# A four-block transformer kernel on one core: GpSimd's bias additions, the inner layer's readouts and the coupling's update as steps of their own, in a new order

## The chip, the core and the metric

The kernel runs on one core of a Trainium2 chip. The metric is the device time of one execution in microseconds (us); lower is better. The engines are TensorE (PE in the profile: matmuls; PEld: its weight loads), VectorE (DVE), ScalarE (ACT), GpSimd (POOL) and SyncE (SP), which issues the DMAs. Each takes its instructions in program order; they wait for each other by semaphores.

## What is computed

The input is 16 sequences of 512 tokens with 256 features, in fp32. Every sequence passes four blocks, each on a normalized input and added back to the state (the kernel folds the last block's factor 0.5 and the middle block's into its weights). Cut to what matters:

```
# L0_attn: latent attention, causal
kv_c = rms(x @ W_kv) * g_kv ; q_c = x @ W_q
k, v, q = kv_c @ W_kdec, kv_c @ W_vdec, q_c @ W_qdec        # 16 heads of 16
k_rope, q_rope = rope(x @ W_krope), rope(q_c @ W_qrope)     # 16 heads of 32
out = softmax(causal([q, q_rope] @ [k, k_rope].T * scale)) @ v @ W_o
# L0_ffn: three rounds of a coupling on the transposed state
for _ in range(3):
    tf = sigmoid(gelu(gelu(gelu(out @ w1 + b1) @ w2 + b2) @ w3 + b3) @ w4 + b4)
    coupling = 0.1 + adaptive_range * (0.7 * gf + 0.3 * tf - 0.5) * 2
    out = out + coupling * twist(out)
# L1_attn: attention with strided keys (strides 1 1 2 2 2 2 4 4 4 4 8 8 8 8 16 16),
#          then layer_norm, @ W1, relu, @ W2, layer_norm
# L1_ffn: s = x @ Win ; sum over 16 inner units of W2 * relu(W1 * s + b1) ; @ Wout + bout
```

The coupling block and the inner block come twice for each sequence: as A and C (coupling, on the input and behind the first attention) and as D and F (inner block, ahead of the second attention and at the end).

## The kernel before

A sequence is called q. Its state lies in X (four tiles of 128 tokens by 256 features), the normalized state in XN and its transpose in XT; each has three slots, for q modulo 3. The stages of a sequence are A (coupling), B (latent attention), C (coupling), D (inner block), E (strided attention), E2 (the two-layer part behind it) and F (inner block). Work of up to four sequences is interleaved: the string TURN lists the steps of one turn as `offset:name.stage.group.part`, and `all_steps` repeats it, turn t giving the steps of q = t + offset. There is no planner at run time: each engine walks through the same list and issues its own part of each step, so the order in TURN is the order on all five queues. A full turn holds every step of the kernel once, and its order decides which work of one sequence lies beside which of another. Where a step has no part for an engine, the engine skips it.

The steps that matter here:
- `xt`: TensorE turns XN (8 matmuls, L476), ScalarE copies it to XT. GpSimd also does the bias additions here, in `transposed` (L1229 on), as instructions over all four tiles: for D and F one (L1233), for E two (L1238, L1239), for E2 two (L1243, L1244). The signal `biased` tells VectorE of each.
- `h1`, `h2`, `h3`, `tf`: the four layers of the coupling net for one round; ScalarE reads out each. In the step `tf` VectorE also moves the state in XT in two halves (`mixed`, L824 to L828). `back` turns the moved state back.
- `stats`, `normal`: VectorE's statistics and normalization (L806, L796, L798, L815), with a power on GpSimd between them (L1217). `latent` and `centre` have such a power too.
- `turn`: a rotation (TensorE's product, VectorE's L865, L866, L868, GpSimd's sum L1254 and a rounded copy L1259); `content`: further products, copied by ScalarE (L1104, L1108, L1114) and rounded by GpSimd (L1268); `max`: scores for the row maxima, reduced by VectorE (L883, L889); `shift`: the maxima turned and subtracted (L895); `exp`: scores and exponentials (L1146), for B with a causal mask by GpSimd (L1275); `sum`: products with the values; `divide`, `att`, `proj`: their end. Banks 0 to 3 of PSUM, as two pairs taken in turn, serve `max`, `exp` and a part of `content` and `v`; banks 5 to 7 the rest.
- `inner`: one product on TensorE; ScalarE then reads it out eight times (L1172) and VectorE adds the eight up in `inner_sum` (L921, then L927 seven times), which ends in `g_ready`; `mout` on TensorE waits for that.
- `up`, `down`: E2's two layers. `down` has VectorE's additions (L949) and needs E2's bias addition; `centre` and `scale` (L960, L969) follow.

A step's name for one sequence is written below as in TURN, exp.B.2.3 for group 2 and key tile 3 of B. A turn that is shown is the one from 1809 to 2030 us of the span.

## Time and profile before

| | |
|---|---|
| median of 3 runs | 3766.49 us (3765.93 to 3772.34) |
| profiled execution, own time | 3778.47 us |
| its span, first to last instruction | 3776.5 us |
| granted TensorE clock, mean | 0.944 |
| TensorE / VectorE / ScalarE / GpSimd busy | 93% / 61% / 51% / 25% |

Busy time is the sum of an engine's instructions over the span. A wait is idle time of an engine ahead of an instruction, put down to whatever released it last. The granted clock is a share of TensorE's full speed of 2.4 GHz; 0.50 is the lower level, 1.2 GHz. In a timeline, neighbouring instructions of one kind are merged into a row, with their number as x; TensorE's rows overlap a little, so the work of a step is best read from one start to the next.

### The profile page before, as it was taken

The numbers are of one execution on the slowest core, as the hardware profiler recorded it, in microseconds if no ns is written. First come the engines' busy times: TensorE is split into PE (matmuls) and PEld (weight loads), VectorE is DVE, ScalarE is ACT, GpSimd is POOL, SyncE is SP. The second block draws the span as 40 slices with busy tenths as digits, with TensorE's granted clock in tenths as the row PEclk, the third lists the DMA queues.
The fourth block names the chain that finished last, engine by engine and source line by source line (L and its number), as shares of the span: only waits on it lengthen the run. The fifth ranks groups of instructions, "written<-read, shape, count | busy, mean of one in ns | idle before, by whom it ended". The sixth has DMA issues, their size and how long they took to land.

```text
span 3776.5 us, 63466 instructions
## 1 busy us (share of the span) xinstructions
PE 3513.1 (93%) x24928; PEld 1994.7 (53%) x24928; DVE 2296.3 (61%) x4778; ACT 1934.1 (51%) x3075; POOL 957.0 (25%) x1037
## 2 busy tenths in 40 slices
PE   5778999999999999999999999999999999999966
PEld 3344555555555555555555555555555565555443
DVE  3446565666756666675666667566666756566442
ACT  2244645546464554646455464645546465554522
POOL 2213132231313223131322313123231313323111
...
GB/s 90 1 1 1 1 1 12 1 12 1 10 3 1 12 1 12 1 7 7 1 12 1 12 1 1 12 1 12 1 12 1 1 12 1 12 1 7 1 6 6
DMA packets 40884, 27.74 MB, mean 7 GB/s; under 512 B 19601, under 2 KB 39697, under 8 KB 40593
## 3 DMA queue, kind: packets, MB, share of 16 engines
...
## 4 chain that ended last, share of the span: by engine, by line
PE 75%; DVE 19%; ACT 3%; issue 2%; POOL 1%; DVEq 0%; ACTq 0%; POOLq 0%
PE ps L465 67%; PE ps L476 7%; DVE G L927 3%; DVE XN L815 2%; DVE stats L806 2%; DVE MX L889 1%; DVE XN L868 1%; DVE MX L883 1%; DVE XN L865 1%; DVE X L969 1%; DVE XN L866 1%; DVE LT L855 1%; DVE mv L796 1%; DVE XN L960 1%; ACT L1146 1%
## 5 line engine op out<-in xcount | busy, mean ns | idle before, releaser
L1146 ACT ACTIVATE PR<-ps 128x1024 f32<-128x1024 f32 (+4 forms) x720 | 540.3, 795 | 604.9 <-PE ps L465 603.4
L465 PE MATMUL ps<-MAT 32*128 32x512 f32 (+5 forms) x4928 | 602.2, 520 | 68.0 <-ACT MAT L1108 52.1
L889 DVE TENSOR_REDUCE MX<-ps 128x2 f32<-128x1024 f32 (+3 forms) x512 | 392.2, 819 | 216.4 <-PE ps L465 214.2
L1217 POOL TENSOR_TENSOR rstd<-var,neg_half 128x4 f32<-128x4 f32 x144 | 150.1, 1042 | 1465.1 <-DVE var L798 1288.9
L465 PEld LDWEIGHTS ps<-MAT 32*128 32x128 f32 (+2 forms) x4928 | 275.7, 203 | 367.0 <-issue 237.5
L883 DVE TENSOR_REDUCE MX<-ps 128x2 f32<-128x1024 f32 (+6 forms) x256 | 219.7, 900 | 299.5 <-PE ps L465 299.5
L465 PE MATMUL ps<-XT,cn_w 128*128 128x256 f32 x1536 | 363.8, 390 | 11.5 <-DVE XT L826 10.8
L465 PE MATMUL ps<-other,cn_w 128*128 128x512 f32 (+2 forms) x1152 | 319.1, 481 | 14.9 <-ACT other L1066 7.6
L465 PEld LDWEIGHTS ps<-XT,cn_w 128*128 128x128 f32 x1536 | 289.7, 194 | 80.3 <-issue 22.4
L1275 POOL TENSOR_SCALAR_AFFINE_SELECT PR<-PR 128x512 f32<-128x512 f32 x256 | 178.9, 699 | 455.5 <-ACT PR L1146 455.1
L1254 POOL TENSOR_TENSOR MAT<-XN 128x512 f32<-128x512 f32 x128 | 163.7, 1279 | 478.4 <-DVE XN L868 478.4
L465 PE MATMUL ps<-HI 32*128 32x256 f32 (+4 forms) x3072 | 218.7, 374 | 45.1 <-DVE MX L889 23.8
L465 PE MATMUL ps<-XT,w_up 128*128 128x512 f32 x512 | 243.3, 610 | 1.0 <-ACT XT L1046 0.9
L815 DVE TENSOR_SCALAR XN<-X,mv,rstd 128x256 f32<-128x256 f32 x384 | 220.3, 635 | 25.3 <-POOL rstd L1217 23.9
L465 PE MATMUL ps<-w_down,other 128*128 128x256 f32 x1024 | 227.4, 380 | 0.0
L824 DVE TENSOR_TENSOR other<-other,XT 128x256 f32<-128x256 f32 x192 | 118.4, 617 | 171.8 <-ACT other L1089 171.8
L465 PEld LDWEIGHTS ps<-HI 32*128 32x128 f32 x3072 | 120.7, 197 | 179.7 <-issue 131.2
L465 PEld LDWEIGHTS ps<-w_down,other 128*128 128x128 f32 x1024 | 193.4, 190 | 33.8 <-issue 7.7
L1268 POOL CAST HI<-MAT 128x512 fp32r<-128x512 f32 (+3 forms) x256 | 156.3, 623 | 198.3 <-ACT MAT L1114 152.0
L1172 ACT ACTIVATE other<-ps,cols 128x512 f32<-128x512 f32 x256 | 174.9, 788 | 58.2 <-PE ps L465 58.2
L465 PE MATMUL ps<-XT,w_qk 128*128 128x512 f32 (+3 forms) x512 | 198.4, 535 | 0.8 <-ACT XT L1049 0.8
L465 PE MATMUL ps<-PR,VB 128*17 128x512 f32 (+3 forms) x2048 | 193.6, 457 | 1.5 <-POOL PR L1275 1.4
...
## 6 DMA issues: line engine op xcount, KB each, us to landing
...
```

The source lines that it names most:

```text
L465: return pe.matmul(dst, lhsT, rhs, start=start, stop=stop, skip_group_check=True)
L476: last = pe.transpose(dst[:, t * P:(t + 1) * P], src(t), ident[:])
L815: last = dve.tensor_scalar(XN[:, c, t, :], src[:, t, :], mv[:, c, t, 0:1], rstd[:, c, t:t + 1], ALU.subtract, ALU.mult)
L824: dve.tensor_tensor(WT[:, a, tok], TF[:, a, tok], XT[:, c, 1, tok], ALU.mult)
L883: last = dve.tensor_reduce(MX[:, t0:t0 + len(parts), at], src[:, :, 0:len(parts) * nk].rearrange("p j (t k) -> p t j k", k=nk), AX_X, ALU.max)
L889: last = dve.tensor_reduce(MX[:, t, at], src[:, :, a:a + nk[pair]], AX_X, ALU.max)
L1146: freed(act.activation(PR[0:m, tile_of((s, q, g, kt)), 2 * pair:2 * pair + 2, q0:T], ps[0:m, b:b + 2, 0:T - q0], ACT.Exp, scale=SCALE[s]), ...
L1172: last = act.activation(U[:, area_of[s], j, :], src, ACT.Relu, scale=c_mw1[:, j:j + 1], bias=c_mb1[:, j:j + 1])
L1217: pool.tensor_tensor(rstd[:, c, :], var[:, c, :], neg_half[:], ALU.pow).then_inc(rstd_ready.sem, 1)
L1254: pool.tensor_tensor(dst, a, b, ALU.add).then_inc(rope_sum.sem, 1)
L1268: pool.tensor_copy(HI[:, content_tile((s, q, g), w, hi=True), 0:n], MAT[:, content_tile((s, q, g), w), 0:n]).then_inc(hi_ready.sem, 1)
L1275: pool.affine_select(out=p, in_=p, compare_op=ALU.is_ge, fill=0.0, base=0, pattern=[[0, 4], [1, P]], channel_multiplier=-1).then_inc(maske ...
```

## The change

Three groups of work get steps of their own, and TURN is written anew with them.
- `bias`: GpSimd's additions leave `xt` and come as bias.D, bias.F, bias.E and bias.E2, each in two parts of two tiles (n = 0, 1). VectorE waits for part 1, and in `down` for the part that it needs. bias.E.1 comes in the next turn.
- `relu`: the eight readouts and sums of an inner layer leave `inner` and come as four steps of two each. `inner` is left with its product.
- `mix`: VectorE's movement of the state leaves `tf` and comes as two steps, one for each half.

Every arithmetic instruction stays, but for the additions of GpSimd, which are now 160 over 128x512 instead of 80 over 128x1024. All other steps keep their content; their order in TURN is new. The strided attention's first group keeps its four rounds of `max`. The string begins at another point of the turn, with the offsets moved along.

```diff
@@ -28,23 +28,27 @@
 MAT_TILES, HI_TILES = 8, 4
 
 TURN = """
--1:exp.E.2.0 1:h3.A.1 0:proj.B 0:stats.C 1:tf.A.1 -1:max.E.1.1 0:normal.C -1:content.E.0 1:h1.A.2 -1:shift.E.1
--1:max.E.0.0 1:h2.A.2 0:xt.C 1:h3.A.2 -1:sum.E.3.0 -1:max.E.0.1 1:tf.A.2 0:h1.C.0 -1:max.E.0.2 -1:divide.E.3
-1:back.A 1:stats.B -1:exp.E.1.0 0:h2.C.0 -1:max.E.0.3 -1:sum.E.2.0 0:h3.C.0 1:normal.B -1:exp.E.1.1 -1:shift.E.0
-0:tf.C.0 -1:sum.E.1.0 1:xt.B -1:exp.E.0.0 -1:divide.E.2 -1:sum.E.1.1 1:latent.B -1:exp.E.0.1 1:turn.B.0.k
--1:sum.E.0.0 -1:exp.E.0.2 -1:sum.E.0.1 1:kvt.B 1:turn.B.0.q 1:content.B.0 -1:exp.E.0.3 -1:divide.E.1 0:h1.C.1
-1:max.B.0.0 -1:sum.E.0.2 0:h2.C.1 1:max.B.0.1 -1:sum.E.0.3 0:h3.C.1 -1:divide.E.0 1:max.B.0.2 1:turn.B.1.k -1:att.E
-1:v.B 1:shift.B.0 0:tf.C.1 1:exp.B.0.0 -1:proj.E 1:turn.B.1.q 1:exp.B.0.1 0:h1.C.2 -1:stats.E2 1:content.B.1
-0:h2.C.2 -1:normal.E2 1:max.B.1.0 0:h3.C.2 -1:xt.E2 1:sum.B.0.0 0:tf.C.2 1:exp.B.0.2 -1:up.0 -1:up.1 1:sum.B.0.1
-1:max.B.1.1 -1:up.2 0:back.C 1:max.B.1.2 0:stats.D 1:sum.B.0.2 -1:up.3 -1:up.4 1:exp.B.0.3 1:shift.B.1 1:turn.B.2.k
-1:exp.B.1.0 1:sum.B.0.3 1:turn.B.2.q 0:normal.D 1:content.B.2 -1:up.5 1:exp.B.1.1 -1:up.6 1:max.B.2.0 0:xt.D -1:up.7
-1:divide.B.0 1:max.B.2.1 0:inner.D -1:down.0 1:max.B.2.2 -1:down.1 -1:centre 1:sum.B.1.0 1:exp.B.1.2 1:shift.B.2
--1:scale 1:sum.B.1.1 1:exp.B.1.3 -1:stats.F 0:mout.D 1:sum.B.1.2 1:exp.B.2.0 -1:normal.F 1:turn.B.3.k 1:sum.B.1.3
-0:stats.E 1:exp.B.2.1 1:sum.B.2.0 -1:xt.F 1:turn.B.3.q 0:normal.E 1:exp.B.2.2 -1:inner.F 1:content.B.3 1:sum.B.2.1
-1:exp.B.2.3 1:sum.B.2.2 1:max.B.3.0 -1:mout.F 1:max.B.3.1 0:xt.E 1:divide.B.1 1:sum.B.2.3 1:max.B.3.2 0:content.E.3
-1:shift.B.3 2:stats.A 2:normal.A 0:v.E 1:exp.B.3.0 0:content.E.2 1:exp.B.3.1 1:sum.B.3.0 2:xt.A 1:exp.B.3.2 2:h1.A.0
-0:max.E.3.0 1:divide.B.2 1:sum.B.3.1 1:exp.B.3.3 2:h2.A.0 0:shift.E.3 0:max.E.2.0 2:h3.A.0 1:sum.B.3.2 1:sum.B.3.3
-2:tf.A.0 0:content.E.1 0:exp.E.3.0 1:divide.B.3 2:h1.A.1 0:shift.E.2 0:max.E.1.0 1:att.B 2:h2.A.1
+1:xt.A -1:max.E.3.0 1:h1.A.0 0:exp.B.3.2 0:divide.B.2 1:h2.A.0 -1:shift.E.3 -1:max.E.2.0 1:h3.A.0 0:sum.B.3.1
+1:tf.A.0 0:sum.B.3.2 1:mix.A.0.0 0:exp.B.3.3 1:mix.A.0.1 -1:shift.E.2 -1:content.E.1 -1:exp.E.3.0 1:h1.A.1
+0:sum.B.3.3 -1:max.E.1.0 1:h2.A.1 0:divide.B.3 -1:content.E.0 1:h3.A.1 0:att.B -1:max.E.1.1 1:tf.A.1 1:mix.A.1.0
+0:proj.B -1:shift.E.1 1:mix.A.1.1 -1:exp.E.2.0 0:stats.C 1:h1.A.2 -1:max.E.0.0 0:normal.C -1:sum.E.3.0 1:h2.A.2
+-1:max.E.0.1 1:h3.A.2 -1:divide.E.3 0:xt.C -1:max.E.0.2 1:tf.A.2 0:h1.C.0 1:mix.A.2.0 1:mix.A.2.1 1:back.A 1:stats.B
+-1:max.E.0.3 0:h2.C.0 -1:sum.E.2.0 0:h3.C.0 -1:exp.E.1.0 1:normal.B -1:divide.E.2 -1:shift.E.0 1:xt.B -1:exp.E.1.1
+0:tf.C.0 0:mix.C.0.0 -1:sum.E.1.0 0:mix.C.0.1 -1:exp.E.0.0 -1:sum.E.1.1 -1:bias.E.1 1:latent.B 1:turn.B.0.k
+-1:exp.E.0.1 -1:sum.E.0.0 -1:exp.E.0.2 -1:sum.E.0.1 1:kvt.B 1:turn.B.0.q 1:content.B.0 -1:exp.E.0.3 0:h1.C.1
+-1:sum.E.0.2 1:max.B.0.0 0:h2.C.1 -1:divide.E.1 1:max.B.0.1 0:h3.C.1 -1:sum.E.0.3 0:tf.C.1 1:max.B.0.2 -1:divide.E.0
+1:turn.B.1.k -1:att.E 1:shift.B.0 1:v.B 0:mix.C.1.0 1:turn.B.1.q 0:mix.C.1.1 1:content.B.1 -1:proj.E 1:exp.B.0.0
+-1:stats.E2 0:h1.C.2 -1:normal.E2 1:max.B.1.0 1:sum.B.0.0 -1:xt.E2 0:h2.C.2 -1:up.0 0:h3.C.2 1:max.B.1.1 0:tf.C.2
+-1:up.1 0:mix.C.2.0 1:exp.B.0.1 -1:bias.E2.0 0:mix.C.2.1 -1:up.2 0:back.C 1:exp.B.0.2 1:sum.B.0.1 -1:up.3 0:stats.D
+1:max.B.1.2 1:sum.B.0.2 0:normal.D -1:up.4 1:exp.B.0.3 1:turn.B.2.k 1:sum.B.0.3 -1:up.5 1:shift.B.1 -1:up.6
+1:turn.B.2.q 1:exp.B.1.0 -1:up.7 1:content.B.2 -1:bias.E2.1 1:exp.B.1.1 0:xt.D 1:max.B.2.0 0:inner.D 0:relu.D.0
+1:divide.B.0 1:max.B.2.1 0:bias.D.0 -1:down.0 0:relu.D.1 1:max.B.2.2 0:relu.D.2 1:sum.B.1.0 0:relu.D.3 -1:down.1
+-1:centre 1:exp.B.1.2 -1:scale 1:sum.B.1.1 1:exp.B.1.3 0:bias.D.1 1:shift.B.2 -1:stats.F 0:mout.D 1:sum.B.1.2
+-1:normal.F 1:exp.B.2.0 1:sum.B.1.3 1:turn.B.3.k 0:stats.E -1:xt.F 1:exp.B.2.1 1:turn.B.3.q 0:normal.E -1:inner.F
+-1:bias.F.0 -1:relu.F.0 -1:relu.F.1 1:sum.B.2.0 1:content.B.3 -1:relu.F.2 1:exp.B.2.2 1:sum.B.2.1 -1:relu.F.3
+1:exp.B.2.3 0:xt.E -1:bias.F.1 1:max.B.3.0 -1:mout.F 1:sum.B.2.2 1:max.B.3.1 0:bias.E.0 0:v.E 1:divide.B.1
+1:max.B.3.2 0:content.E.3 1:shift.B.3 2:stats.A 1:sum.B.2.3 1:exp.B.3.0 0:content.E.2 2:normal.A 1:exp.B.3.1
+1:sum.B.3.0
 """
 
 
...
@@ -915,24 +918,26 @@
                     for n in range(2):
                         read_out(dve, "proj", s, q, n)
 
-                def inner_sum(s, q):
+                def inner_sum(s, q, i):
                     a = area_of[s]
-                    dve.wait_ge(inner_ready.sem, inner_ready.at(s, q, 0))
-                    link(dve.tensor_scalar(G[:, a, :], U[:, a, 0, :], c_mw2[:, 0:1], c_mb2, ALU.mult, ALU.add))
-                    for j in range(1, 8):
+                    for j in (2 * i, 2 * i + 1):
                         if j < 7:
                             dve.wait_ge(inner_ready.sem, inner_ready.at(s, q, j))
                         else:
                             read_out(dve, "s", s, q)
-                        last = dve.scalar_tensor_tensor(G[:, a, :], U[:, a, j, :], c_mw2[:, j:j + 1], G[:, a, :],
-                                                        ALU.mult, ALU.add)
+                        if j == 0:
+                            last = dve.tensor_scalar(G[:, a, :], U[:, a, 0, :], c_mw2[:, 0:1], c_mb2, ALU.mult, ALU.add)
+                        else:
+                            last = dve.scalar_tensor_tensor(G[:, a, :], U[:, a, j, :], c_mw2[:, j:j + 1], G[:, a, :],
+                                                            ALU.mult, ALU.add)
                         if j < 7:
                             link(last)
-                    last.then_inc(g_ready.sem, 1)
-                    dve.wait_ge(g_ready.sem, g_ready.at(s, q))
+                    if i == 3:
+                        last.then_inc(g_ready.sem, 1)
+                        dve.wait_ge(g_ready.sem, g_ready.at(s, q))
 
                 def features_added(s, q):
-                    dve.wait_ge(biased.sem, biased.at(s, q))
+                    dve.wait_ge(biased.sem, biased.at(s, q, 1))
                     for n in range(2):
                         src = when_full(dve, "mout", s, q, n).rearrange("p (t d) -> p t d", t=2)
                         x = X[:, q % CH, 2 * n:2 * n + 2, :]
...
@@ -942,8 +947,7 @@
 
                 def down_added(q, n):
                     c = q % CH
-                    if n == 0:
-                        dve.wait_ge(biased.sem, biased.at("HB", q))
+                    dve.wait_ge(biased.sem, biased.at("HB", q, n))
                     src = when_full(dve, "down", q, n).rearrange("p (t d) -> p t d", t=2)
                     acc = XN[:, c, 2 * n:2 * n + 2, :]
                     freed(dve.tensor_tensor(acc, src, acc, ALU.add), "down", q, n)
...
@@ -1166,14 +1170,15 @@
                             last = act.activation(ATT[:, f, :], src, ACT.Identity, bias=c_vb[:, f:f + 1])
                         freed(last, "att", s, q, f)
 
-                def inner(s, q):
+                def inner(s, q, i):
                     src = when_full(act, "s", s, q)
-                    for j in range(8):
+                    for j in (2 * i, 2 * i + 1):
                         last = act.activation(U[:, area_of[s], j, :], src, ACT.Relu, scale=c_mw1[:, j:j + 1],
                                               bias=c_mb1[:, j:j + 1])
                         if j < 7:
                             last.then_inc(inner_ready.sem, 1)
-                    freed(last, "s", s, q)
+                    if i == 3:
+                        freed(last, "s", s, q)
 
                 for name, *a in STEPS:
                     if name == "xt":
...
@@ -1226,22 +1231,20 @@
                     linked[0] += 1
                     pool.wait_ge(pool_step, linked[0])
 
-                def transposed(s, q):
-                    c = q % CH
+                def bias(s, q, n):
+                    x, xn = (t[:, q % CH, 2 * n:2 * n + 2, :] for t in (X, XN))
                     if s in "DF":
                         pool.wait_ge(xn_ready.sem, xn_ready.at(s, q))
-                        pool.tensor_tensor(X[:, c], X[:, c], bcast(bout_d), ALU.add).then_inc(biased.sem, 1)
-                    elif s == "E":
-                        pool.wait_ge(xn_ready.sem, xn_ready.at(s, q))
-                        for f in range(KT):
-                            when_full(pool, "xt", s, q, f)
-                        pool.tensor_tensor(XN[:, c], XN[:, c], bcast(bout_e), ALU.add).then_inc(biased.sem, 1)
-                        pool.tensor_tensor(X[:, c], X[:, c], bcast(beta_r), ALU.add).then_inc(biased.sem, 1)
-                    elif s == "E2":
-                        for f in range(KT):
-                            when_full(pool, "xt", s, q, f)
-                        link(pool.tensor_tensor(XN[:, c], XN[:, c], bcast(gamma_r), ALU.mult))
-                        pool.tensor_tensor(XN[:, c], XN[:, c], bcast(betab2_r), ALU.add).then_inc(biased.sem, 1)
+                        pool.tensor_tensor(x, x, bcast(bout_d), ALU.add).then_inc(biased.sem, 1)
+                        return
+                    for f in range(KT):
+                        when_full(pool, "xt", s, q, f)
+                    if s == "E":
+                        pool.tensor_tensor(xn, xn, bcast(bout_e), ALU.add).then_inc(biased.sem, 1)
+                        pool.tensor_tensor(x, x, bcast(beta_r), ALU.add).then_inc(biased.sem, 1)
+                    else:
+                        link(pool.tensor_tensor(xn, xn, bcast(gamma_r), ALU.mult))
+                        pool.tensor_tensor(xn, xn, bcast(betab2_r), ALU.add).then_inc(biased.sem, 1)
 
                 def rotated(q, g, w):
                     a, b = rope_parts(q)
```

The hunks left out adapt the signals, the waits and the dispatch of the steps; `mixed` gets v as an argument in place of its loop.

## Rows read from the trace of the kernel before

**Rows 1.** The page's part 1: busy time, share, instructions.

```profile
PE 3513.1 (93%) x24928; PEld 1994.7 (53%) x24928; DVE 2296.3 (61%) x4778; ACT 1934.1 (51%) x3075; POOL 957.0 (25%) x1037
```

**Rows 2.** TensorE's waits, whole span: us in total, times, longest.

```profile
PE ps L465 <- ACT MAT L1108: 52.1, 14, 3.7
...
PE ps L465 <- DVE G L927: 26.6, 16, 7.1
```

**Rows 3.** Timeline of TensorE: start us, us, instruction, [idle before <-releaser].

```profile
1876.96 7.17 PE L465 MATMUL ps<-w_down,other 128*128 128x256 f32 x32
1884.06 1.05 PE L465 MATMUL ps<-PR,VB 128*17 128x512 f32 x8
...
1908.92 0.71 PE L465 MATMUL ps<-MAT 32*128 32x128 f32 x8 [3.72 <-ACT MAT L1108]
1909.57 0.87 PE L465 MATMUL ps<-PR,VB 128*17 128x256 f32 x8
...
1913.26 3.65 PE L465 MATMUL ps<-m_out,G 128*128 128x256 f32 x8 [1.41 <-DVE G L927]
...
1919.06 0.41 PE L465 MATMUL ps<-PR,VB 128*17 128x128 f32 x8
```

**Rows 4.** Windows of 5 us: engines' busy time (x), granted clock, DMA.

```profile
1910.00:1915.00 5.00, 3.59 (x33) 2.12 (x29) 4.86 (x6) 0.07 (x1) 0.95 (x2) 0.50 0.02 5
1915.00:1920.00 5.00, 4.69 (x57) 3.17 (x58) 4.04 (x7) 1.55 (x3) 1.13 (x1) 0.84 0.26 93
...
1930.00:1935.00 5.00, 5.00 (x20) 2.14 (x12) 0.00 (x0) 2.20 (x3) 0.71 (x2) 0.63 0.00 0
```

**Rows 5.** Timeline of VectorE around the inner layer of F.

```profile
1857.63 3.05 DVE L815 TENSOR_SCALAR XN<-X,mv,rstd 128x256 f32<-128x256 f32 x4
...
1870.77 5.48 DVE L927 SCALAR_TENSOR_TENSOR G<-other,cols,G 128x512 f32<-128x512 f32 x7 [0.20 <-ACT other L1172]
...
1888.48 2.04 DVE L969 SCALAR_TENSOR_TENSOR X<-XN,rstd,X 128x256 f32<-128x256 f32 x4
...
1901.39 5.09 DVE L815 TENSOR_SCALAR XN<-X,mv,rstd 128x256 f32<-128x256 f32 x4
...
1906.97 6.24 DVE L927 SCALAR_TENSOR_TENSOR G<-other,cols,G 128x512 f32<-128x512 f32 x7
```

**Rows 6.** Timeline of GpSimd, the same stretch.

```profile
1857.91 1.26 POOL L1254 TENSOR_TENSOR MAT<-XN 128x512 f32<-128x512 f32 x1 [0.81 <-DVE XN L868]
...
1901.31 2.35 POOL L1233 TENSOR_TENSOR X<-X,rows 128x1024 f32<-128x1024 f32 x1
1903.61 1.33 POOL L1254 TENSOR_TENSOR MAT<-XN 128x512 f32<-128x512 f32 x1
```

**Rows 7.** Timeline of VectorE: normal.E2, the coupling's last movement, normal.B.

```profile
1828.36 1.71 DVE L815 TENSOR_SCALAR XN<-XN,mv,rstd 128x256 f32<-128x256 f32 x4 [1.59 <-POOL rstd L1217]
...
1989.97 0.42 DVE L828 TENSOR_TENSOR XT<-XT,other 128x256 f32<-128x256 f32 x1
...
1998.18 1.37 DVE L815 TENSOR_SCALAR XN<-X,mv,rstd 128x256 f32<-128x256 f32 x4
```

**Rows 8.** Timeline of ScalarE: a second layer's readout, a table load.

```profile
1831.07 0.69 ACT L1066 ACTIVATE other<-ps,cols 128x512 f32<-128x512 f32 x1 [1.22 <-PE ps L465]
...
1945.96 1.28 ACT L1146 ACT_TABLE_LOAD   x1 [1.34 <-PE ps L465]
```

**Rows 9.** Timeline of TensorE: max.E, h1.C.0, back.A and xt.B.

```profile
1984.85 0.50 PE L465 MATMUL ps<-HI 32*128 32x512 f32 x4
...
1985.91 3.92 PE L465 MATMUL ps<-XT,cn_w 128*128 128x256 f32 x16
...
1991.03 1.04 PE L476 MATMUL ps<-ident,XT 128*128 128x128 f32 x8
...
2001.41 1.09 PE L476 MATMUL ps<-ident,XN 128*128 128x128 f32 x8
```

**Rows 10.** Timeline of TensorE: exp.B.0.0 behind shift.B.0.

```profile
1815.93 2.02 PE L465 MATMUL ps<-MAT 32*128 32x512 f32 x16 [0.15 <-DVE MAT L895]
```

47 lines of the change are left out of this document (23 added, 24 removed).

## The prediction

> **What bounds the kernel now.** I read the page's busy line first: TensorE is busy 93% of the span, VectorE 61%, ScalarE 51%, GpSimd 25% [rows 1]. So a new order can win only what TensorE idles or what it loses to a low clock, and it can lose by letting TensorE run into results that are not there yet. The list of TensorE's waits says where it idles in the steady part: 52.1 us behind ScalarE's copy of L1108 in 14 waits, and 26.6 us behind the inner layer's sum, L927, in 16 waits of which two are at the ends [rows 2]. Fourteen is my count of full turns. The timeline of one turn shows both in one place: TensorE stops for 3.72 us in the second half of exp.B.2.3, at 1905.2, and for 1.41 us before mout.F, at 1911.9 [rows 3]. The windows show the granted clock fall to 0.50 between 1910 and 1915, behind these stops, and once more to 0.63 between 1930 and 1935 [rows 4].
>
> The cause lies on VectorE. Between the end of down.1 on TensorE (1876.96 + 7.17 = 1884.13 [rows 3]) and the end of the sum for F (1906.97 + 6.24 = 1913.21 [rows 5]) it is hardly ever idle: last layer added, centre, scale, stats.F, mout.D, normal.F, two rotations, stats.E, normal.E, eight sums. TensorE's mout.F starts at 1913.26, so this stretch, 29.1 us, is as long as VectorE's chain. It holds about 24.0 us of TensorE's work (29.13 - 3.72 - 1.41).
>
> Part of that chain is GpSimd in VectorE's way. normal.E takes 5.09 us for its four instructions, beside GpSimd's bias addition for F (2.35 us from 1901.31) and the rotation's sum behind it (1.33 us from 1903.61) [rows 5, 6]. With only a rotation's sum beside them (1.26 us from 1857.91) the same four take 3.05 us [rows 5, 6]; with nothing beside them 1.37 us [rows 7]. So a two-input addition on GpSimd holds up VectorE's next such instruction for its whole length. The Trainium skill says the same (SBUF — State Buffer, "Who interferes with whom": "Whoever issues first gets the shared pair for the whole instruction"), and adds that the order of issue, not the kind of operation, decides who blocks; the trace agrees as far as VectorE is the one that blocks, and shows no two-input GpSimd addition that had to wait for a chain of L927.
>
> **The change, part by part.** No arithmetic is added. Signals, the splits of mix and relu, and the reworked loops leave the instructions as they are; they cost nothing by themselves, and the busy engines show it, since all but TensorE are under two thirds. GpSimd's 80 wide additions become 160 of half the width; at about 1.27 us each, the length of the other half-wide addition (1.26 [rows 6]) against 2.35 / 2, that is 0.1 us more apiece on an engine that is idle 75% of the time, so nothing. The new places are what matters. I add up TensorE's work between neighbours of a dependency in the old and the new order, per turn.
>
> Term 1, VectorE's chain from down.1 to mout.F. Its list is the same in the new order, only scale and shift.B.2 change places. What changes is what GpSimd does beside it. F's addition is halved and bias.F.0 stands behind turn.B.3.q: normal.E now meets the rotation's sum (3.05 us) and the first half, about 0.9 us of it, so 5.09 becomes 3.95: -1.1. bias.D.1 now stands behind exp.B.1.3's mask, and so beside scale, which takes 2.04 us from 1888.48 [rows 5]; one of its instructions waits most of a 1.27 us addition: +0.9. Before, D's addition ran long before. bias.F.1 and bias.E.0 (two additions) stand right behind exp.B.2.3's mask. ScalarE now does that exponential behind relu.F.3 and not behind the whole inner layer, so I put the mask some 3 us ahead of the sum's end, and the first of these additions stops one L927: +1.1. If the next two get in between as well, +1.2 more, and if none comes in time, 0. I take -1.1 + 0.9 + 1.1 = +0.9. Bounds: -4.1, if GpSimd always lets VectorE pass (normal.E back to 1.7 us, L927 at the 5.48 that it took for D with nothing beside it, instead of 6.24 [rows 5]), and +3.3.
>
> Term 2, work that leaves this stretch. It is VectorE's, so TensorE's work in it is free. sum.B.1.0 (1.05 us) moves ahead of down.1 and sum.B.2.2 (0.87) behind mout.F, [rows 3], while xt.E (like each xt 1.09 [rows 9]) moves in. TensorE pays 1.05 + 0.87 - 1.09 = +0.8; I take +0.7, since the 0.87 is one of the slow clock.
>
> Term 3, gaps that become too short elsewhere. Each need is read in the old turn:
> - A second layer's output needs 0.69 us on ScalarE (1831.07 to 1831.76) and the third layer follows at once [rows 8]. In the new order only max.E.0.1 stands between h2.A.2 and h3.A.2, a step of 0.50 us with its overlap [rows 9], some 0.4 without: +0.4.
> - h2.A.0 and h3.A.0 keep their gap, but ScalarE now changes tables around exp.B.3.2, which is longer than exp.B.3.3 was; a change is 1.28 us [rows 8]: +0.4.
> - From the start of h1.C.0 behind tf.A.2 (1985.91 [rows 9]) to the end of the last movement of the state, L828 (1989.97 + 0.42 [rows 7]), it is 4.5 us; back.A now comes after h1.C.0 alone, 3.92 us [rows 9]: +0.5. h1.A.1 to h2.A.1 shrinks to 0.8 us, a sum and a maximum: +0.15.
> - shift.B.3 to exp.B.3.0 keeps sum.B.2.3 alone (0.41 us [rows 3]). Where 0.75 stood between, TensorE already waited 0.15 us for L895 [rows 10]: +0.4, and that 0.15 is gone.
> - xt.D to inner.D keeps one small step: +0.2.
> These make 0.4 + 0.4 + 0.65 + 0.4 - 0.15 + 0.2 = 1.9.
> Two more go through GpSimd's queue. bias.E.1, two additions, now stands right behind the power for stats.B, so normal.B, 1.37 us when free [rows 7], waits for both. In the old turn its end came 7.5 us behind back.A's (1999.55 - 1992.07 [rows 7, 9]), with 0.7 for a division that now goes elsewhere; 6.8 + up to 1.5 for the additions meet 7.2 us of TensorE's work, where 9.3 stood (1992.07 to 2001.41 [rows 9]): up to 1.1. And the power for stats.E2 stands behind exp.B.0.0's mask, while proj.E to xt.E2 falls from 10.9 to 7.3 us; normal.E2 ended 1830.07 in the old turn after a wait of 1.59 us for that power [rows 7]: up to 0.6. These ride on when GpSimd gets there, so I take half, 0.8. Against it, two short waits of the old turn, 0.2 each, should go: -0.4. Term 3: +2.3, between +1.0 and +3.3.
>
> Term 4, the clock. A stop of some 2 to 4 us before mout.F stays, and v.E now comes 3 us behind it instead of 10, so two falls may become one. The old turn lost about 2.5 us of work at 0.50 and 0.84 (half of 3.59 and a sixth of 4.69 [rows 4]). Bounds -2.3 and +1.5; I take 0.
>
> Sum per turn: 0.9 + 0.7 + 2.3 + 0 = +3.9 us. Over 14 turns +55 us. The head and the tail, where all engines idle, I leave at nothing, 10 us either way. The profiled execution has 3776.5 us of span and 3778.5 in all, 12 above the median of 3766.5; the difference is carried to the median: 3821.
>
> **The rivals.**
> Rival A, faster: GpSimd is the one that waits. If halved additions slip in between VectorE's instructions, by the rule on the order of issue, the chain falls to 25 us, where TensorE's own work is the bound: term 1 is -4.1, term 3 only its lower +1.0, and the clock no longer falls behind the stop, -2.3. With term 2 that is -4.7 a turn, -66 us, 3701. It decides from the point where fewer than about two of the five additions near the chain block it. For it: no wait of 3.7 us behind the inner layer's eight readouts is needed any more, since content.B.3 comes after four of them. Against it: every turn shows VectorE blocked whole.
> Rival B, nearly even: only the gain on normal.E comes, the other additions miss VectorE and the gaps cost their lower bound: -1.1 + 0.7 + 1.0 = +0.6 a turn, +8 us, 3775. The edit then only moves idle time about.
> Rival C, much slower: all additions block, the gaps cost 3.3 and the short rows of v.E behind the stop hold the clock down: 3.3 + 0.7 + 3.3 + 1.5 = +8.8, +123 us, 3890.
>
> **How the numbers follow.** The forecast has 0.45 and a range of its own from 3795 to 3850; A has 0.25, B 0.20, C 0.10. A measurement of this kernel tells about 0.2%, 7.5 us, from nothing, so "same" is 3759 to 3774. B lies at that edge and is split: 0.05 faster, 0.12 same, 0.03 slower. Faster 0.30, same 0.12, slower 0.58. For 8 in 10 the range has to take in the middle of A and leaves out the far half of A and most of C: 3700 to 3870.
>
> **What would show it.** Right: a stop before mout.F of 2 us or more and the sum for F at 6.5 us or more beside bias.F.1; scale above 2.5 us; waits of 0.3 to 1 us at h3.A, back.A, exp.B.3.0 and xt.B; a turn of about 224.7 us where it is now 220.9. Wrong: L927 waits under 0.5 us a turn and no fall of the clock near mout.F, then it is A; or the distance from down.1 to mout.F under 26 us.

## The result and the profile after

| | before | after |
|---|---|---|
| median (range) | 3769.41 us (3765.93 to 3781.89, 4 runs) | 3895.55 us (3893.86 to 3896.26, 4 runs) |
| ratio, 95% interval | | 1.0322 (1.0304 to 1.0341) |
| span of the profiled execution | 3776.5 us | 3894.3 us |
| granted TensorE clock, mean | 0.944 | 0.944 |

The changed kernel is 3.2% slower. The forecast was 3821, so the direction was right and the size was not: the time lies 25 us above the upper end of the range, beside rival C's 3890.

The page's busy line of the changed kernel:

```profile
PE 3569.4 (92%) x24928; PEld 2022.2 (52%) x24928; DVE 2326.9 (60%) x4778; ACT 1902.3 (49%) x3047; POOL 978.2 (25%) x1133
```

The span is 117.8 us longer, and no engine is fuller than before [rows 1]. TensorE's 56 us more of busy time are not more work: its instructions are as many. The rest is idle time. I split the span at the products of `kvt` on TensorE, one a turn. The 13 steady turns between them take 229.8 us on average and took 221.3, which is 111.3 us in all; the part ahead of them is 9.6 us shorter and the part behind 16.1 us longer (111.3 - 9.6 + 16.1 = 117.8). So the steady turn has to be explained, +8.6 us.

TensorE's waits in the changed kernel (total us, times, longest); lines after L806 or so stand 3 to 5 further down than before, L927 is now L931, L895 L898, L815 L820, L969 L973:

```profile
PE ps L470 <- DVE G L931: 83.5, 16, 7.2
PE ps L481 <- DVE XN L820: 63.8, 25, 19.8
PE ps L470 <- DVE MAT L898: 36.8, 33, 2.1
```

The wait for the sum of the inner layer was 26.6 us and is 83.5; that for ScalarE's copy L1108, 52.1 before [rows 2], is gone, and 36.8 us stand at L898, which had 3.5 before. The timeline of TensorE through the stretch that [rows 3] show of before:

```profile
1921.21 7.17 PE L470 MATMUL ps<-w_down,other 128*128 128x256 f32 x32
...
1936.32 2.02 PE L470 MATMUL ps<-MAT 32*128 32x512 f32 x16 [2.10 <-DVE MAT L898]
...
1941.26 1.09 PE L481 MATMUL ps<-ident,XN 128*128 128x128 f32 x8 [0.67 <-DVE XN L820]
...
1959.53 3.63 PE L470 MATMUL ps<-m_out,G 128*128 128x256 f32 x8 [3.71 <-DVE G L931]
```

From the end of down.1 (1921.21 + 7.17 = 1928.38) to mout.F it is 31.15 us, where it was 29.13. The stop of 3.72 us in exp.B.2.3 is gone; in its place stand 2.10 at exp.B.2.0, 0.67 at xt.F and 3.71 before mout.F. This is the better sort of turn, three of the thirteen steady ones. In the other ten the same stretch takes 33.5 us (here 2156.05 to 2189.51):

```profile
2148.88 7.17 PE L470 MATMUL ps<-w_down,other 128*128 128x256 f32 x32
...
2163.98 3.60 PE L470 MATMUL ps<-MAT 32*128 32x512 f32 x16 [2.10 <-DVE MAT L898]
...
2189.51 3.78 PE L470 MATMUL ps<-m_out,G 128*128 128x256 f32 x8 [5.28 <-DVE G L931]
```

Here exp.B.2.0 takes 3.60 us for the 2.02 of the other turn: the granted clock is 0.54 over that step, and 1.00 over the same step of the better turn; the window around it shows 0.73.

```profile
2165.00:2170.00 5.00, 5.00 (x29) 1.79 (x24) 3.37 (x12) 2.43 (x3) 1.38 (x2) 0.73 0.02 5
```

VectorE in the better turn, to be read against [rows 5], and in the last two lines in the other turn:

```profile
1932.23 3.31 DVE L973 SCALAR_TENSOR_TENSOR X<-XN,rstd,X 128x256 f32<-128x256 f32 x4
...
1939.49 1.72 DVE L820 TENSOR_SCALAR XN<-X,mv,rstd 128x256 f32<-128x256 f32 x4
...
1947.03 3.71 DVE L820 TENSOR_SCALAR XN<-X,mv,rstd 128x256 f32<-128x256 f32 x4
...
1951.52 7.96 DVE L931 SCALAR_TENSOR_TENSOR G<-other,cols,G 128x512 f32<-128x512 f32 x7
...
2170.00 0.69 DVE L868 TENSOR_TENSOR XN<-ps,rope_sin 128x512 f32<-128x512 f32 x1 [1.47 <-PE ps L470]
...
2180.40 9.06 DVE L931 SCALAR_TENSOR_TENSOR G<-other,cols,G 128x512 f32<-128x512 f32 x7
```

GpSimd beside it, against [rows 6]. L1238 is the addition for D and F, L1243 and L1244 are E's two; L1278 is the mask of exp.B.2.3:

```profile
1933.43 1.44 POOL L1238 TENSOR_TENSOR X<-X,rows 128x512 f32<-128x512 f32 x1
...
1949.27 1.31 POOL L1238 TENSOR_TENSOR X<-X,rows 128x512 f32<-128x512 f32 x1
...
1954.87 0.73 POOL L1278 TENSOR_SCALAR_AFFINE_SELECT PR<-PR 128x512 f32<-128x512 f32 x1 [1.09 <-ACT PR L1150]
1955.57 1.69 POOL L1238 TENSOR_TENSOR X<-X,rows 128x512 f32<-128x512 f32 x1
1957.23 1.70 POOL L1243 TENSOR_TENSOR XN<-XN,rows 128x512 f32<-128x512 f32 x1
1958.89 1.71 POOL L1244 TENSOR_TENSOR X<-X,rows 128x512 f32<-128x512 f32 x1
```

Scale takes 3.31 us instead of 2.04, normal.E 3.71 instead of 5.09, and the sum for F 7.96 or 9.06 instead of 6.24: bias.F.1 and the first addition of bias.E.0 lie beside its end. In the second turn VectorE waits 1.47 us for the rotation's product, which TensorE's slow exp.B.2.0 has delayed; so the sum starts later against GpSimd's queue, and bias.E.0's other addition lies beside it too (2187.20 to 2188.90, the sum's end 2189.46).

### The profile page after: what moved, and what is told of

Read it like the earlier page. It is cut to its first block, busy times and chain, and to the rows that moved or that the text cites. A ratio compares the mean times of both kernels' runs of the same rounds, so it can differ in the third digit from the quotient of the medians.

```text
span 3894.3 us, 63581 instructions
## 1 busy us (share of the span) xinstructions
PE 3569.4 (92%) x24928; PEld 2022.2 (52%) x24928; DVE 2326.9 (60%) x4778; ACT 1902.3 (49%) x3047; POOL 978.2 (25%) x1133
## 4 chain that ended last, share of the span: by engine, by line
PE 72%; DVE 20%; ACT 5%; issue 2%; POOL 0%; DVEq 0%; ACTq 0%; POOLq 0%
PE ps L470 66%; PE ps L481 5%; DVE G L931 3%; DVE MX L892 3%; DVE XN L820 2%; DVE stats L811 1%; ACT PR L1150 1%; DVE X L973 1%; DVE MX L886 1%; DVE XN L868 1%; DVE XN L869 1%; DVE XN L871 1%; DVE XN L964 1%; DVE MAT L898 1%; ACT other L1070 1%
## 5 line engine op out<-in xcount | busy, mean ns | idle before, releaser
L470 PE MATMUL ps<-MAT 32*128 32x512 f32 (+5 forms) x4928 | 618.2, 508 | 48.0 <-DVE MAT L898 36.8
L470 PEld LDWEIGHTS ps<-MAT 32*128 32x128 f32 (+2 forms) x4928 | 290.0, 197 | 327.9 <-issue 167.8
L1278 POOL TENSOR_SCALAR_AFFINE_SELECT PR<-PR 128x512 f32<-128x512 f32 x256 | 169.9, 666 | 699.7 <-ACT PR L1150 691.7
L470 PE MATMUL ps<-XT,w_qk 128*128 128x512 f32 (+3 forms) x512 | 222.6, 587 | 0.0
L931 DVE SCALAR_TENSOR_TENSOR G<-other,cols,G 128x512 f32<-128x512 f32 x224 | 216.6, 967 | 9.8 <-ACT other L1176 3.6
L470 PEld LDWEIGHTS ps<-w_down,other 128*128 128x128 f32 x1024 | 192.2, 190 | 38.7 <-issue 12.9
L820 DVE TENSOR_SCALAR XN<-X,mv,rstd 128x256 f32<-128x256 f32 x384 | 194.0, 568 | 26.4 <-POOL rstd L1222 25.0
L470 PEld LDWEIGHTS ps<-other,cn_w 128*128 128x128 f32 (+2 forms) x1152 | 114.6, 170 | 162.5 <-issue 101.2
```

Source lines behind the costliest of these rows:

```text
L470: return pe.matmul(dst, lhsT, rhs, start=start, stop=stop, skip_group_check=True)
L820: last = dve.tensor_scalar(XN[:, c, t, :], src[:, t, :], mv[:, c, t, 0:1], rstd[:, c, t:t + 1], ALU.subtract, ALU.mult)
L931: last = dve.scalar_tensor_tensor(G[:, a, :], U[:, a, j, :], c_mw2[:, j:j + 1], G[:, a, :], ALU.mult, ALU.add)
L1278: pool.affine_select(out=p, in_=p, compare_op=ALU.is_ge, fill=0.0, base=0, pattern=[[0, 4], [1, P]], channel_multiplier=-1).then_inc(maske ...
```

## The experiments

All experiments on the changed code keep its arithmetic, but for the first. Steps are moved in TURN; a diff shows the places with the neighbours needed to find them. Turns and stretches without a row are worked out from the starts of TensorE's steps, as means of nine of the thirteen steady turns, the same nine in every kernel.

**Are the additions to blame, or the order?** Three kernels. The first keeps the new order and cuts every bias addition to the first of the 256 columns of each tile. That leaves the biases of the other columns out, 255 of 256 and not the 127 of 128 of the text below.

```diff
-                    return v.unsqueeze(1).broadcast_to([P, 2, C])
+                    return v[:, 0:1].unsqueeze(1).broadcast_to([P, 2, 1])
...
-                    x, xn = (t[:, q % CH, 2 * n:2 * n + 2, :] for t in (X, XN))
+                    x, xn = (t[:, q % CH, 2 * n:2 * n + 2, 0:1] for t in (X, XN))
```

> The changed kernel with GpSimd's 160 bias additions cut to one column each: 127 of 128 columns of every addition are left out, all waits and signals stay. Theory G (the additions stand in VectorE's way beside the chain from down.1 to mout.F): scale falls from 3.3 to about 2.0 us, normal.E from 3.7 to 3.1, the seven L931 from 8.0 (and more) to 6.3; the chain loses some 4 us a turn, and the kernel ends near 3820. Rival O (the order itself: TensorE's gaps between dependent steps became too short, whatever GpSimd does): 3880 or more. Rival K (the clock, which falls twice or three times a turn): the chain shortens but the kernel stays above 3860.

Measured: 3773.16 us, ratio to before 0.9991 (0.9981 to 1.0000). An addition takes 0.24 us instead of 1.31, and nothing is left of the 3.2%. Theory G is borne out in kind, O and K are not; but G's 3820 was 47 us too high. The stretch from down.1 to mout.F lost 5.4 us a turn, not 4, and 3 us went outside it: 2.4 between mout.F and xt.A, and 0.8 behind xt.A. TensorE is at the lower clock for 6.6 us of the turn, against 16.0.

The second keeps all the work of the change and moves the additions for D, F and E to places where VectorE runs no chain that TensorE waits for:

```diff
-... 0:bias.D.0 -1:down.0 ... 1:exp.B.1.3 0:bias.D.1 ...
+... 0:bias.D.0 0:bias.D.1 -1:down.0 ... 1:exp.B.1.3 ...
-... -1:normal.F ... -1:inner.F -1:bias.F.0 ... 0:xt.E -1:bias.F.1 ...
+... -1:normal.F -1:bias.F.0 -1:bias.F.1 ... -1:inner.F ... 0:xt.E ...
-... 0:bias.E.0 0:v.E ... 0:content.E.2 ... -1:bias.E.1 1:latent.B ...
+... 0:v.E ... 0:content.E.2 0:bias.E.0 0:bias.E.1 ... 1:latent.B ...
```

> The changed kernel with the additions at other places and nothing else: bias.D.1 right behind bias.D.0, both parts of F right behind normal.F (ahead of the rotation turn.B.3.k, where VectorE reads PSUM), both parts of E behind content.E.2, where VectorE idles. Theory G: as good as leaving the additions out, within 0.5%: about 3820. Rival O: no more than 0.5% off the changed kernel, 3876 or more. If only a part comes back, the additions find other instructions to block.

Measured: 3780.67 us, ratio 1.0013 (1.0003 to 1.0022), 115 us less than the changed kernel. Its VectorE in the same stretch:

```profile
1884.36 2.30 DVE L973 SCALAR_TENSOR_TENSOR X<-XN,rstd,X 128x256 f32<-128x256 f32 x4
...
1898.27 3.35 DVE L820 TENSOR_SCALAR XN<-X,mv,rstd 128x256 f32<-128x256 f32 x4
...
1902.40 5.98 DVE L931 SCALAR_TENSOR_TENSOR G<-other,cols,G 128x512 f32<-128x512 f32 x7
```

The three operations are shorter than in the changed kernel by 1.0, 0.4 and 2.0 to 3.1 us, and the stretch from down.1 to mout.F falls from 33.0 to 28.0. Here too G's 3820 was too high, by 39 us.

The third is the other half: the changed code, its halved additions, but the order before, each new step where its work was. It stands for the code alone.

> The changed kernel's code with the old order: bias, relu and mix steps stand right behind the xt, inner and tf steps that they came from, so only the halving of the additions is left of the change. Theory G and rival O agree: the splitting costs nothing, 3760 to 3777; where F's first half meets normal.E, its half length may save up to 1 us a turn. If the splitting itself costs (more instructions and signals on GpSimd), 3780 or more.

Measured: 3770.61 us, ratio 0.9992 (0.9980 to 1.0003). Splitting the steps and halving the additions costs nothing, as the prediction had it. The new order without its additions beside the chain, 3773 or 3781, is within 0.3% of the kernel before too. That is not yet the price of the order: the kernel before has an addition of its own beside normal.E. The two are told apart below, where the old order is run with F's additions moved.

**Which addition?** Each of the three moves above alone, on the changed kernel: the first, the second and the third pair of lines of the last diff.

> The changed kernel with only bias.D.1 moved, to behind bias.D.0. Theory G: scale falls from 3.3 to 2.3 us, TensorE's stop before exp.B.2.0 from 2.1 to 1.1 us, and with it the early fall of the clock that lengthened two turns in three by 2.3 us: 2.5 us a turn, 3860. If that stop is not what starts the early fall, only 1 us a turn, 3882.

> The changed kernel with only F's two additions moved, to behind normal.F. Theory G: normal.E falls from 3.7 to 3.1 us and one blocked L931 (0.9 us) goes; E's first two additions still stand behind exp.B.2.3's mask and move up into the sum. 1 to 2 us a turn, 3870 to 3882. If F is the only one that matters: 3800.

> The changed kernel with only E's additions moved, to behind content.E.2. Theory G: the sum for F loses the one or two blocks by bias.E.0 (0.9 to 1.8 us), and xt.B its wait of 0.5 us behind bias.E.1: 2 to 3 us a turn, and the turns in which the clock falls early and a third addition is caught no longer differ: 3850 to 3865. If E does not matter, within 0.2% of 3896.

| moved alone | time, us | ratio to before (95%) | stretch down.1 to mout.F | turn |
|---|---|---|---|---|
| none (the change) | 3895.55 | 1.0322 (1.0304 to 1.0341) | 33.0 | 230.1 |
| D's second addition | 3849.68 | 1.0216 (1.0200 to 1.0231) | 30.2 | 226.8 |
| F's two | 3868.74 | 1.0266 (1.0251 to 1.0281) | 30.7 | 228.4 |
| E's four | 3848.09 | 1.0210 (1.0193 to 1.0227) | 31.3 | 226.8 |
| all three | 3780.67 | 1.0013 (1.0003 to 1.0022) | 28.0 | 221.9 |

The three gains are 46, 27 and 47 us, 120 together, against 115 for all at once (in ratios 1.1, 0.6 and 1.1% against 3.1%). That the times add up is in part chance: the stretch itself loses 2.8, 2.3 and 1.7 us alone, 6.8 together, and only 5.0 for all at once, where the rest comes from mout.F to xt.A. E gives more than its stretch (1.7 us) because bias.E.1 also stood ahead of the power for stats.B: the wait of 0.51 us at xt.B goes with it. F's stretch is 2.3 us shorter, but 0.7 of it goes again between mout.F and xt.A. D came out 10 us below the 3860 expected, E and F 2 and 1 us below their ranges. With D's addition moved, the stop at exp.B.2.0 is 1.09 us instead of 2.10, and the stretch is 30.2 us in all thirteen turns: the early fall of the clock is gone. With E's moved the two sorts of turn stay, 30.3 and 31.7 us, which E's expectation had ruled out.

**Does the place of shift.B.2 matter?** It stood ahead of scale before; in the change it waits behind a scale that bias.D.1 lengthens.

```diff
-... 1:exp.B.1.2 -1:scale 1:sum.B.1.1 1:exp.B.1.3 0:bias.D.1 1:shift.B.2 ...
+... 1:exp.B.1.2 1:shift.B.2 -1:scale 1:sum.B.1.1 1:exp.B.1.3 0:bias.D.1 ...
```

> The changed kernel, with one step moved: shift.B.2 stands ahead of scale again, as in the order before, where the change has it behind scale and bias.D.1. In the changed kernel TensorE stops 2.1 us a turn at exp.B.2.0, and that stop ends with shift.B.2's subtraction on VectorE, which is queued behind a scale that bias.D.1 has lengthened. T (the place of shift.B.2 makes this stop, and the stop brings the fall of the clock ahead of xt.F in two turns of three, which lets one more addition into the chain of sums): the stop goes, every turn's stretch from down.1 to mout.F comes to the 31.2 us of the good turn of three, on average 1.8 us less, and the whole to 3860 to 3875. R (VectorE's chain alone sets the start of mout.F, and it is as long in either order): the stop at exp.B.2.0 goes, the stop ahead of mout.F grows by the same 2 us, and the time stays within 8 us of the changed kernel's 3895.

Measured: 3868.03 us, ratio 1.0261 (1.0242 to 1.0280), 27.5 us less than the change, the size that T gave. The stop at exp.B.2.0 goes, and one of 2.50 us comes at xt.F, where TensorE waits for the same chain one step on. One of the turns in which the clock is low behind it, TensorE and VectorE:

```profile
2157.44 1.78 PE L481 MATMUL ps<-ident,XN 128*128 128x128 f32 x8 [2.50 <-DVE XN L820]
2159.15 2.51 PE L470 MATMUL ps<-MAT 32*128 32x384 f32 x16
```

```profile
2149.59 2.92 DVE L973 SCALAR_TENSOR_TENSOR X<-XN,rstd,X 128x256 f32<-128x256 f32 x4
...
2162.83 0.69 DVE L868 TENSOR_TENSOR XN<-ps,rope_sin 128x512 f32<-128x512 f32 x1 [1.39 <-PE ps L470]
...
2169.16 8.00 DVE L931 SCALAR_TENSOR_TENSOR G<-other,cols,G 128x512 f32<-128x512 f32 x7
```

The stretch is 30.6 or 32.2 us, where it was 31.2 or 33.5. T is right that the third block goes: the sum is 8.0 us in either sort of turn, and never 9.06. It is wrong that the slow turns end: the fall of the clock only comes behind another stop and still delays VectorE by 1.4 us. R is right that stops change place, and wrong on the time.

The same move and the three of the additions together:

> The changed kernel with all its additions for D, E and F in places where no chain of VectorE's is beside them (as in the kernel that took 3781), and with shift.B.2 ahead of scale. There a stop of 1.1 us a turn was left at exp.B.2.0. T: with the chain off the limit this stop costs its whole length, so 14 times 0.8 to 1.1 us go: 3765 to 3770. R: VectorE's chain still ends last, so nothing is won: 3777 to 3785.

Measured: 3779.30 us, ratio 1.0023 (1.0013 to 1.0032). R held: the 1.09 us at exp.B.2.0 turned up at xt.F, whose stop grew from 0.33 to 1.34 us, and nothing was won in the time. The stretch is 27.6 us for 28.0, and still set by VectorE.

**Do the places cost as much in the old order?** The old order with the additions where the change puts them: D.0 behind relu.D.0, D.1 behind exp.B.1.3, F.0 behind normal.E, F.1 behind exp.B.2.3, E.0 behind xt.E, E.1 behind stats.B, E2.1 behind content.B.2. The cut shows the places of D and F.

```diff
-... 0:bias.D.0 0:bias.D.1 ... 1:exp.B.1.3 ... -1:xt.F -1:bias.F.0 -1:bias.F.1 ... 0:normal.E ... 1:exp.B.2.3 ...
+... 0:bias.D.0 ... 1:exp.B.1.3 0:bias.D.1 ... -1:xt.F ... 0:normal.E -1:bias.F.0 ... 1:exp.B.2.3 -1:bias.F.1 ...
```

> The order before, with the new steps in the places where the old kernel did their work, but with the halved additions where the change puts them: bias.D.1 behind exp.B.1.3, bias.F.0 behind normal.E, bias.F.1 behind exp.B.2.3, bias.E.0 behind xt.E, bias.E.1 behind stats.B, bias.E2.1 behind content.B.2. T (the places of the additions make the loss, whatever the order of the rest): scale is held up as in the change (3.3 us instead of 2.0) and the sum for F by one or two additions (7 to 8 us instead of 6.2), while normal.E is freed of most of its 1.5; the stretch from down.1 to mout.F comes to 30.5 to 31.5 us instead of 29.2, and the whole to 3800 to 3825. R (the loss needs the new order, in which scale and shift.B.2 have changed places and exp.B.2.3 stands behind relu.F.3): within 10 us of the kernel before, since scale has slack behind shift.B.2 and exp.B.2.3's mask comes late.

Measured: 3791.06 us, ratio 1.0054 (1.0037 to 1.0071), between the two ranges. In the old order the same places cost 0.5% against the kernel before, not 3.2%. Its VectorE and GpSimd:

```profile
1892.36 3.05 DVE L973 SCALAR_TENSOR_TENSOR X<-XN,rstd,X 128x256 f32<-128x256 f32 x4
...
1906.12 3.70 DVE L820 TENSOR_SCALAR XN<-X,mv,rstd 128x256 f32<-128x256 f32 x4
...
1910.63 7.25 DVE L931 SCALAR_TENSOR_TENSOR G<-other,cols,G 128x512 f32<-128x512 f32 x7
```

```profile
1915.64 1.69 POOL L1238 TENSOR_TENSOR X<-X,rows 128x512 f32<-128x512 f32 x1
...
1924.09 1.27 POOL L1243 TENSOR_TENSOR XN<-XN,rows 128x512 f32<-128x512 f32 x1 [6.76 <-PE ps L481]
```

Against [rows 5] scale +1.0, normal.E -1.4, the sum +1.0, and the stretch 30.1 us for the 29.2 of the old order: +0.9. The turn is 222.0 us against 220.2. The additions for E start 6.2 us after the sum has ended. What the new order adds beside the chain is that they come at once behind bias.F.1, because xt.E has moved ahead of mout.F, and that shift.B.2 sits behind scale.

**Is there a better kernel in it?** The old order with F's additions behind normal.F, so that nothing wide lies beside normal.E:

```diff
-... -1:normal.F ... -1:xt.F -1:bias.F.0 -1:bias.F.1 ...
+... -1:normal.F -1:bias.F.0 -1:bias.F.1 ... -1:xt.F ...
```

> The old order as in the run before, with both parts of F's addition moved from behind xt.F to behind normal.F, ahead of turn.B.3.k. Theory G: normal.E falls from 5.1 to 3.1 us and the chain from down.1 to mout.F from 29.1 to about 27.1, 2 us a turn: 3740. Rival W (TensorE's 3.7 us behind ScalarE's eight readouts is a stop of its own, so VectorE's chain is not the bound): under 10 us, 3760.

Measured: 3739.70 us, ratio 0.9907 (0.9892 to 0.9921): faster than both kernels by 0.9% and 4.0%. The turn falls from 220.2 us in the old order with the changed code to 218.5. Its TensorE:

```profile
1892.97 1.22 PE L470 MATMUL ps<-MAT 32*128 32x128 f32 x8 [3.71 <-ACT MAT L1112]
...
1896.53 2.86 PE L470 MATMUL ps<-m_out,G 128*128 128x256 f32 x8
```

The stop before mout.F is gone; the sum ends at 1895.06, 1.5 us ahead of need. G's 3740 came, but half of it by another way. The stretch from down.1 to mout.F falls by 0.9 us, not 2, because TensorE's stop behind ScalarE's copy stays, as W had said, though W's 3760 did not come; the other 0.9 goes between mout.F and xt.A, and the time at the lower clock falls from 12.9 to 8.9 us a turn. With this kernel the order and the places of the additions can be told apart (ratio to before; in brackets the turn):

| | additions off VectorE's chain | where the change puts them |
|---|---|---|
| old order | 0.9907 (218.5 us) | 1.0054 (222.0 us) |
| new order | 1.0013 (221.9 us) | 1.0322 (230.1 us) |

"Off the chain" means F's additions moved in the old order, and those of D, E and F in the new one. So the new order costs 1.1% by itself, and the places 1.5% in the old order and 3.1% in the new one. The new order looked free against the kernel before only because it was measured with an addition less in the way.

What is left in the kernel of 3740 us is the 3.71 us in exp.B.2.3, behind ScalarE's copy. Two kernels built on it go at that. The first:

```diff
-... -1:relu.F.0 -1:relu.F.1 -1:relu.F.2 -1:relu.F.3 1:content.B.3 1:sum.B.2.1 1:exp.B.2.3 ...
+... -1:relu.F.0 1:content.B.3 -1:relu.F.1 -1:relu.F.2 1:sum.B.2.1 1:exp.B.2.3 -1:relu.F.3 ...
```

> The old order with F's additions behind normal.F, as in the last run of the old order, and one idea of the change taken over: content.B.3 stands behind relu.F.0 and exp.B.2.3 ahead of relu.F.3, so that ScalarE frees the pair of banks before its eight readouts are done. Theory V (VectorE's chain, now 27.1 us, bounds the stretch): TensorE's 3.7 us before exp.B.2.3 goes, 2 to 3 us come back before mout.F; 1 us a turn and a clock that falls less, 3715 to 3730. Rival W (ScalarE's readouts bound it): 3 us a turn and more, 3690. If the stops only change place: 3740.

Measured: 3740.04 us, ratio 0.9926 (0.9911 to 0.9941). Stops of 2.04 us at max.B.3.0 and 1.6 to 2.2 at mout.F take the place of the one of 3.71: the stops only change place, the third of the outcomes named. The second:

```diff
-... 1:exp.B.2.2 -1:inner.F ... -1:relu.F.3 1:content.B.3 ...
+... 1:exp.B.2.2 1:content.B.3 -1:inner.F ... -1:relu.F.3 ...
```

> The order before with F's halved additions behind normal.F (the kernel that took 3740), and with content.B.3 ahead of inner.F instead of behind it. There a stop of 3.7 us a turn is left in exp.B.2.3, because ScalarE copies content.B.3 only after the eight readouts of F; the sum for F ends 1.5 us ahead of mout.F. T (that stop is TensorE's limit there, and VectorE's chain follows 1.5 us behind): the copy comes before the readouts, the stop shrinks to 2 us or less, the stretch from down.1 to mout.F from 28.3 to about 27 us, and the whole to 3715 to 3730. R (the stop only changes place, as with the other order of the readouts that took 3740): the readouts start 1.3 us later, the sum ends later by as much, mout.F waits for it, and the time stays at 3735 to 3745.

Measured: 3741.19 us, ratio 0.9921 (0.9907 to 0.9936). R held, in another place than it said. The copy is in time, and the next step waits for a PSUM pair that ScalarE's exponentials, now the ones behind the readouts, free late:

```profile
1893.83 0.74 PE L470 MATMUL ps<-HI 32*128 32x512 f32 x8 [4.20 <-ACT PR L1150]
```

In all three kernels the stretch is 27.3 to 28.3 us and the time 3740. ScalarE has eight readouts, two copies and the exponentials to do there, and whichever is put last has TensorE waiting. That its list is the limit, whatever its order, is how I read this; no run shortens the list.

## Why the prediction was half right

**What bounds the kernel: right for one of the two stops.** VectorE's chain from down.1 to mout.F sets the stretch, and GpSimd's additions beside it decide its length. The kernel with F's additions moved shows it from the side of gain, the three single moves from the side of loss. But I laid the 3.72 us in exp.B.2.3 to that chain as well, and it is ScalarE's: with normal.E 1.9 us shorter it stays at 3.71 and then sets the stretch. The stop of 1.41 us before mout.F that I read is also not the usual one; it is 0.71 in ten of the thirteen turns.

The steady turn by stretches, from the starts of TensorE's steps (means of nine turns), with the kernel of old order and changed code between, and last the change with its three additions away:

| stretch, us | before | code alone | after | additions away |
|---|---|---|---|---|
| latent.B to end of down.1 | 99.8 | 99.8 | 102.3 | 102.3 |
| end of down.1 to mout.F | 29.2 | 29.2 | 33.0 | 28.0 |
| mout.F to xt.A | 24.9 | 23.8 | 26.0 | 23.6 |
| xt.A to latent.B | 67.4 | 67.5 | 68.9 | 68.1 |
| turn | 221.3 | 220.2 | 230.1 | 221.9 |

**Term 1, +0.9 a turn: the step that failed.** The stretch grew by 3.8 us: by 2.0 in three of the thirteen turns and by 4.3 in the other ten. The forecast counted one L927 stopped behind exp.B.2.3's mask where two or three were, and put the new place of shift.B.2 at nothing. By its parts:
- normal.E: 3.95 us forecast, -1.1; measured 3.71, -1.4. Right.
- bias.D.1 beside scale: +0.9 forecast, +1.3 measured (3.31 against 2.04). But I took it as a length of the chain only. I wrote that scale and shift.B.2 change places and gave that no price; TensorE stops 2.10 us at exp.B.2.0 for it, 1.09 with bias.D.1 away, and in ten turns of thirteen the clock is down behind that stop. With D's addition moved it is down in none.
- the sum for F: +1.1 forecast for one block, +1.2 more if E's two get in. It took +1.7 in the better turns, with two blocks, and +2.8 in the others, with three; each makes 1.63 us of an L931 of 0.75. The place of the mask was about right: it starts at 1954.87, and unblocked the sum would have ended near 1957.5 (an estimate: its start, 1951.52, and the 5.98 us that it takes with the additions away), 2.6 us later, where I had put 3. What failed is the count behind it. The first block moves the sum's end by 0.9 us, so the next addition, which stands right behind the first and starts 1.7 us after it, finds the last L931 not yet begun. That followed from the forecast's own figures: with the mask 3 us ahead, two blocks belonged in the sum, not one.

Together the parts make +1.6 and +2.7. In the ten turns VectorE's wait of 1.47 us for the rotation's product comes on top, behind the slow exp.B.2.0.

In the old order the same places of the additions lengthen the stretch by +0.9, by scale +1.0, normal.E -1.4 and the sum +1.0. So the price of a block was right and the number of blocks was not. The upper bound of +3.3 failed as well. Its parts as I gave them add up to +2.1 only (-1.1 + 0.9 + 1.1 + 1.2), and even +3.3 left out that a stop, the clock and the next block feed each other there; I had bounded the clock in a term of its own.

**Term 2, +0.7: right.** sum.B.1.0, 1.05 us, now lies ahead of down.1; between mout.F and xt.A, with the additions away, the rest is 23.6 against 23.8, the 0.87 of sum.B.2.2 less the 1.09 of xt.E. Together +0.8.

**Term 3, +2.3: right in sum, with wrong parts.** The first stretch grew by 2.5, of which 1.05 are term 2, and the last by 1.4. Between mout.F and xt.A, exp.B.3.0 waits 0.38, and 0.28 that max.B.3.2 waited is gone: 1.4 + 1.4 + 0.4 - 0.3 = +2.9, at the upper part of its bounds. TensorE's timeline of the changed kernel, at h3.A.2, back.A and xt.B, which were named, and at att.E and shift.B.0, which were not:

```profile
2031.45 0.65 PE L470 MATMUL ps<-other,cn_w 128*64 128x256 f32 x4 [0.35 <-ACT other L1070]
...
2039.13 1.06 PE L481 MATMUL ps<-ident,XT 128*128 128x128 f32 x8 [0.33 <-DVE XT L831]
...
2047.67 1.28 PE L481 MATMUL ps<-ident,XN 128*128 128x128 f32 x8 [0.51 <-DVE XN L820]
...
2082.37 1.09 PE L481 MATMUL ps<-ident,ATN 128*128 128x128 f32 x8 [0.36 <-DVE ATN L907]
2083.79 0.63 PE L481 MATMUL ps<-ident,MX 128*128 128x128 f32 x4 [0.32 <-DVE XN L869]
```

h3.A.2 was put at 0.4 and is 0.35, back.A 0.5 and 0.33, xt.B 0.55 and 0.51, exp.B.3.0 0.4 and 0.38, h2.A.1 0.15 and 0.20 (means of the steady turns); h3.A.0, put at 0.4 more, waits 0.17 more than it did. inner.D and xt.E2 did not come. Not foreseen were att.E 0.35, shift.B.0 0.32 and three of 0.2 to 0.3 at `max` and exp.B.2.2; against them kvt's 0.61 went. TensorE's recorded idle time grew from 6.1 to 10.9 us a turn, so about half of the +8.6 is in such rows; the rest is work that moved into slow stretches and steps that got longer.

**Term 4, the clock, 0: wrong.** The time of a turn at the lower clock is about 15 us before and 16 after, and the mean 0.944 both times, but it lies on other work. Windows of the changed kernel (length; PE, PEld, DVE, ACT, POOL busy; clock; DMA):

```profile
1955.00:1960.00 5.00, 1.29 (x25) 0.79 (x26) 4.86 (x5) 0.71 (x2) 5.00 (x4) 0.95 0.00 0
1960.00:1965.00 5.00, 5.00 (x42) 3.22 (x42) 3.54 (x5) 0.00 (x0) 0.60 (x1) 0.71 0.03 9
...
1970.00:1975.00 5.00, 5.00 (x56) 3.17 (x56) 2.63 (x6) 0.54 (x3) 0.24 (x1) 0.50 0.04 15
```

It falls behind the stop before mout.F, as before [rows 4], and again at 1970, where content.E.3 takes 4.63 us; on average that step takes 4.3 us against 2.3. The stretch from mout.F to xt.A is +1.1 longer than before, and 2.3 of the 4.3 in the stretch ahead come only in the turns with a slow exp.B.2.0. In the thirteen steady turns there are 26 falls before and 36 after: they became more, not fewer. With the three additions away the time at the lower clock is 6.8 us a turn. The +1.1 itself is no firm number: the code alone, in the old order, has 23.8 there for 24.9, so two executions of the same work differ by as much, and the whole of it against 23.8 would be +2.2.

**The rivals.** A (additions slip in between) is refuted by the sum's 7.96 to 9.06 us. B's time, 3775, is where both kernels of the new order without the blocks end, 3773 and 3781; there the order's own cost and the cleared normal.E about cancel, as B had it. C is what happened in kind, with blocks, gaps and clock all at the dear end, at 8.8 a turn against a measured 8.6 to 8.8; it had 0.10. Its term 1 of 3.3 was no sum of its parts, which make 2.1. Its time over the whole, 3890, came near partly by chance: it counted 14 turns and nothing at the ends, and it is 13 turns, with -9.6 and +16.1 us at the ends. Of the signs that the prediction named, the stop before mout.F of 2 us or more, scale above 2.5, the sum at 6.5 or more and the four waits came; the turn is 229.8 us where it named 224.7.
